# A gated delta rule layer with a mixture of experts on one core: how the first pairs of each inverse are selected, how its first two levels get their transposed halves, and a new order of work on all engines

## The reference

```
mixed = silu(causal_conv(x @ w_qkv, conv_w))         # 4 taps; q, k: 16 heads of 128; v: 32 heads of 128
z = x @ w_z;  beta = sigmoid(x @ w_b);  g = -exp(A_log) * softplus(x @ w_a + dt_bias)
q, k = l2norm(q) * 128**-0.5, l2norm(k)              # each key head serves two value heads
for t in range(512):                                 # per sequence and value head, state 128 x 128
    state = state * exp(g[t])
    delta = (v[t] - k[t] @ state) * beta[t]
    state = state + outer(k[t], delta)
    o[t] = q[t] @ state
o = rmsnorm(o * silu(z)) * gamma
x = layernorm(x + o @ w_out)
```

## Time and profile before

| what | value |
|---|---|
| median of three runs | 2604.27 us |
| the profiled execution | 2603.33 us |
| its span, first to last instruction | 2601.6 us |
| around the span | 1.7 us |
| mean granted clock of TensorE | 0.967 of full speed |
| busy: PE, DVE, POOL, ACT | 91%, 76%, 54%, 52% |

### The profile page before, as it was taken

How to read it: one execution, slowest core, us unless ns; L and a number is a source line. 1 busy time by engine, 2 the same in 40 slices (tenths; PEclk the granted TensorE clock), 3 DMA queues, 4 the chain that set the end, 5 groups by cost and what they waited for, 6 DMA issues and landing times.

```text
span 2601.6 us, 54037 instructions
## 1 busy us (share of the span) xinstructions
PE 2379.1 (91%) x20078; PEld 1827.1 (70%) x20078; DVE 1987.8 (76%) x3452; ACT 1359.8 (52%) x4123; POOL 1417.4 (54%) x1198
## 2 busy tenths in 40 slices
PE   5899999999999999999999999999999999997998
PEld 3677777777777777777777777777777777775665
DVE  4778778777887777877778777887778877784665
ACT  3555565555555555555555555555555555553110
POOL 3465655656555665556655566555666556662000
PEclk9899999999999999999999999999999999998999
DMA  3011010101010100101010101101010110001000
GB/s 125 34 42 34 33 42 34 42 34 47 28 50 25 50 34 26 50 29 46 34 42 34 46 29 35 41 34 50 26 50 26 50 34 26 34 2 71 25 9 17
DMA packets 32100, 98.47 MB, mean 38 GB/s; under 512 B 4320, under 2 KB 9824, under 8 KB 31584
## 3 DMA queue, kind: packets, MB, share of 16 engines
q1 hardware_dynamic: 31840, 95.02, 10.6%
HBM read 92.39 MB, written 2.62 MB: 37 GB/s over the span
## 4 chain that ended last, share of the span: by engine, by line
PE 70%; POOL 16%; DVE 8%; issue 4%; ACT 0%; POOLq 0%; DMA 0%; DVEq 0%; SPq 0%; ACTq 0%
PE bank L870 18%; POOL XT L810 11%; PE bank L894 11%; PE bank L992 4%; PE bank L924 4%; PE bank L965 4%; PE bank L914 4%; PE bank L991 4%; PE bank L482 4%; DVE X L1152 3%; PE bank L953 3%; POOL mhiT L796 3%; PE bank L975 2%; PE bank L930 2%; PE bank L878 2%
## 5 line engine op out<-in xcount | busy, mean ns | idle before, releaser
L1125 DVE SCALAR_TENSOR_TENSOR conv<-bank,cw_all,conv 128x511 f32<-128x511 f32 (+2 forms) x768 | 571.4, 744 | 19.6 <-ACT conv L1030 6.0
L870 PE MATMUL bank<-xT,w_kh 128*128 128x512 f32 x1024 | 537.7, 618 | 2.7 <-ACT kraw L1058 1.8
L1075 ACT ACTIVATE X<-bank 128x512 f16<-128x512 f32 x384 | 228.9, 596 | 449.2 <-PE bank L924 435.8
L1161 DVE TENSOR_TENSOR N<-bank,lev 128x512 f16<-128x512 f32 x384 | 264.8, 690 | 107.3 <-PE bank L914 97.6
L914 PEld LDWEIGHTS bank<-X,mhiT 128*128 128x128 f16 x3072 | 132.3, 98 | 262.8 <-DVE X L1152 179.6
L750 POOL TENSOR_SCALAR ss<-ssum 128x4 f32<-128x4 f32 x64 | 14.6, 228 | 544.2 <-ACT sqj L1052 544.2
L894 PE MATMUL bank<-w_kh,xT 128*128 128x256 f32 x1024 | 310.0, 442 | 0.0
L914 PE MATMUL bank<-X,mhiT 128*128 128x64 f16 x3072 | 154.3, 194 | 165.6 <-DVE X L1152 164.2
L810 POOL TENSOR_SCALAR_AFFINE_SELECT XT<-mhiT 128x1024 f16<-128x1024 f16 x64 | 287.2, 4487 | 4.4
L1007 PE MATMUL bank<-wo,ogT 128*128 128x256 f32 x1024 | 246.8, 384 | 0.0
L1152 DVE STREAM_TRANSPOSE X<-XT 128x1024 f16<-128x1024 f16 x64 | 79.7, 1245 | 208.4 <-POOL XT L815 208.4
(11 more groups left out here) (160 smaller groups left out, 5859.7 us busy)
## 6 DMA issues: line engine op xcount, KB each, us to landing
egb<-rows SPq DMA_DIRECT2D x64, 512.0 KB, 3.6
ecb<-rows SPq DMA_DIRECT2D x64, 512.0 KB, 3.7
w_kh<-w_heads SPq DMA_DIRECT2D x16, 768.0 KB, 4.8
wo_raw<-w_out SPq DMA_DIRECT2D x16, 256.0 KB, 5.1
xT<-x_cols SPq DMA_DIRECT2D x4, 512.0 KB, 5.9
qT<-x_rows SPq DMA_DIRECT2D x4, 512.0 KB, 3.6
xT<-gate_up SPq DMA_DIRECT2D x1, 2048.0 KB, 7.5
out<-og SPq DMA_DIRECT2D x4, 512.0 KB, 3.0
```

The source lines that it names most:

```text
L870: mm = pe.matmul(PB[j % 2][:, :], w[:, k, g * P:(g + 1) * P], xT[:, k, b * SEQ:(b + 1) * SEQ], start=(k == 0), stop=(k == KT - 1))
L1075: act.activation(blocks(X[:, :, :], i, 0), packed(IB[i % 2], i), ACT.Copy).then_inc(s_x, 1)
L1125: dve.scalar_tensor_tensor(conv[:, g, m:], PB[j % 2][:, 0:SEQ - m], cw_all[:, head, g * TAPS + 3 - m:g * TAPS + 4 - m], conv[:, g, m:], op ...
L1161: dve.tensor_tensor(blocks(N[:, i], i, 0), packed(IB[1 - i % 2], i), blocks(lev[:, 1 + i:2 + i, :], i, 0).broadcast_to(shape), ALU.mult).t ...
```

## The change

1. `pairs`: the first select wrote all columns of XT with a pattern of three dimensions whose innermost had two elements, and the second then put ones into the odd columns, after a wait on the first. Now two selects of 512 elements in each partition write the even and the odd columns from the matching columns of `mhiT`, with the comparison `is_ge` and fill 0. Neither reads what the other writes, and the semaphore between them is gone. `x0` waits for both. What stands in XT is the same as before.
2. `TURNED` goes from 2 to 0: at levels 0 and 1 the transposed half comes from `growt` on PE and ACT, and DVE's two transposes `turned` are gone.
3. `ORDER` is new on all four engines. PE's round now begins with `write` of chunk 0 and `products` 1. `products` 0 of body k + 2 is the last item of the round before, and `solve` 0 stands ahead of it. `m`, `mhi`, `pairs`, `x0` and `join` 0 have moved from the end of the round to its beginning (ahead 1 in place of 2), and `solve`, `read` and `write` of chunk 1 from the end of the round before to this one. The three gate items of a body but the first stand between `products` and `join` 0.

```diff
--- before.py
+++ after.py
@@ -24,40 +24,41 @@
 NX = NE + 1
 NQ = 4
 Q_BETA, Q_EG, Q_KEYS, Q_EEND = range(NQ)
-TURNED = 2
+TURNED = 0
 COLS_OF = (1, 0, 2, 3)
 
 ORDER = {
     "tensor": [
-        ("read", 2, 0), ("growx", 0, 1), ("gate", 1, 1), ("gate", 2, 1), ("join", 1, 1), ("gate", 3, 1),
-        ("growx", 1, 1), ("proj", 0, 2), ("proj", 1, 2), ("join", 2, 1), ("solve", 2, 0), ("proj", 2, 2),
-        ("growx", 2, 1), ("growt", 2, 1), ("proj", 3, 2), ("join", 3, 1), ("write", 2, 0), ("out", 0, 0),
-        ("growx", 3, 1), ("ktp", 0, 2), ("read", 3, 0), ("growt", 3, 1), ("join", 4, 1), ("out", 1, 0),
-        ("growx", 4, 1), ("solve", 3, 0), ("growt", 4, 1), ("out", 2, 0), ("join", 5, 1), ("out", 3, 0),
-        ("growx", 5, 1), ("growt", 5, 1), ("proj", 4, 2), ("newton", 0, 1), ("ktp", 1, 2), ("proj", 5, 2),
-        ("newton", 1, 1), ("finish", 0, 1), ("proj", 6, 2), ("finish", 1, 1), ("proj", 7, 2), ("solve", 0, 1),
-        ("products", 0, 2), ("write", 0, 1), ("products", 1, 2), ("turn", 0, 0), ("read", 1, 1), ("turn", 1, 0),
-        ("project", 0, 0), ("project", 1, 0), ("solve", 1, 1), ("project", 2, 0), ("project", 3, 0), ("vtp", 0, 2),
-        ("write", 1, 1), ("vtp", 1, 2), ("join", 0, 2), ("gate", 0, 2),
+        ("write", 0, 0), ("products", 1, 1), ("gate", 1, 1), ("read", 1, 0), ("gate", 2, 1), ("gate", 3, 1),
+        ("proj", 0, 2), ("solve", 1, 0), ("join", 0, 1), ("proj", 1, 2), ("write", 1, 0), ("growx", 0, 1),
+        ("growt", 0, 1), ("proj", 2, 2), ("read", 2, 0), ("proj", 3, 2), ("solve", 2, 0), ("join", 1, 1),
+        ("out", 0, 0), ("write", 2, 0), ("growx", 1, 1), ("growt", 1, 1), ("ktp", 0, 2), ("read", 3, 0),
+        ("join", 2, 1), ("out", 1, 0), ("solve", 3, 0), ("growx", 2, 1), ("out", 2, 0), ("out", 3, 0),
+        ("growt", 2, 1), ("join", 3, 1), ("proj", 4, 2), ("ktp", 1, 2), ("proj", 5, 2), ("growx", 3, 1),
+        ("growt", 3, 1), ("proj", 6, 2), ("join", 4, 1), ("proj", 7, 2), ("turn", 0, 0), ("growx", 4, 1),
+        ("growt", 4, 1), ("turn", 1, 0), ("project", 0, 0), ("join", 5, 1), ("project", 1, 0), ("growx", 5, 1),
+        ("growt", 5, 1), ("project", 2, 0), ("vtp", 0, 2), ("newton", 0, 1), ("newton", 1, 1), ("project", 3, 0),
+        ("finish", 0, 1), ("finish", 1, 1), ("vtp", 1, 2), ("gate", 0, 2), ("solve", 0, 1), ("products", 0, 2),
     ],
     "scalar": [
-        ("u", 1, 0), ("silu", 2, 1), ("silu", 3, 1), ("vals", 0, 1), ("vals", 1, 1), ("growx", 0, 1), ("zs", 0, 1),
-        ("growx", 1, 1), ("zs", 1, 1), ("tap", 0, 2), ("u", 2, 0), ("growx", 2, 1), ("growt", 2, 1), ("silu", 0, 2),
-        ("tap", 1, 2), ("growx", 3, 1), ("squares", 0, 2), ("growt", 3, 1), ("kraw", 0, 2), ("u", 3, 0),
-        ("growx", 4, 1), ("growt", 4, 1), ("power", 0, 0), ("growx", 5, 1), ("silu", 1, 2), ("growt", 5, 1),
-        ("squares", 1, 2), ("tap", 2, 2), ("power", 1, 0), ("u", 0, 1), ("tap", 3, 2), ("turn", 0, 0), ("turn", 1, 0),
+        ("growt", 4, 0), ("silu", 3, 1), ("growx", 5, 0), ("growt", 5, 0), ("vals", 0, 1), ("u", 0, 0),
+        ("vals", 1, 1), ("zs", 0, 1), ("zs", 1, 1), ("u", 1, 0), ("tap", 0, 2), ("growt", 0, 1), ("growx", 0, 1),
+        ("u", 2, 0), ("silu", 0, 2), ("tap", 1, 2), ("growx", 1, 1), ("growt", 1, 1), ("kraw", 0, 2),
+        ("squares", 0, 2), ("u", 3, 0), ("growx", 2, 1), ("power", 0, 0), ("silu", 1, 2), ("growt", 2, 1),
+        ("power", 1, 0), ("squares", 1, 2), ("tap", 2, 2), ("growx", 3, 1), ("growt", 3, 1), ("tap", 3, 2),
+        ("turn", 0, 0), ("growx", 4, 1), ("turn", 1, 0), ("silu", 2, 2),
     ],
     "vector": [
-        ("join", 2, 1), ("conv", 0, 2), ("conv", 1, 2), ("conv", 2, 2), ("join", 3, 1), ("s", 2, 0), ("conv", 3, 2),
-        ("join", 4, 1), ("rhs", 3, 0), ("og", 0, 0), ("conv", 4, 2), ("conv", 5, 2), ("join", 5, 1), ("scan", 0, 2),
-        ("scan", 1, 2), ("res", 0, 1), ("og", 1, 0), ("res", 1, 1), ("tt", 0, 1), ("tt", 1, 1), ("conv", 6, 2),
-        ("conv", 7, 2), ("conv", 8, 2), ("s", 0, 1), ("conv", 9, 2), ("m", 0, 2), ("m", 1, 2), ("rhs", 1, 1),
-        ("conv", 10, 2), ("conv", 11, 2), ("p", 0, 2), ("p", 1, 2), ("x0", 0, 2), ("acc", 0, 0), ("s", 1, 1),
-        ("join", 0, 2), ("rhs", 2, 1), ("turned", 0, 2), ("join", 1, 2), ("acc", 1, 0), ("turned", 1, 2),
+        ("m", 0, 1), ("m", 1, 1), ("s", 0, 0), ("p", 0, 1), ("p", 1, 1), ("rhs", 1, 0), ("x0", 0, 1), ("join", 0, 1),
+        ("s", 1, 0), ("conv", 0, 2), ("conv", 1, 2), ("rhs", 2, 0), ("conv", 2, 2), ("join", 1, 1), ("s", 2, 0),
+        ("conv", 3, 2), ("rhs", 3, 0), ("join", 2, 1), ("og", 0, 0), ("conv", 4, 2), ("conv", 5, 2), ("og", 1, 0),
+        ("join", 3, 1), ("conv", 6, 2), ("conv", 7, 2), ("join", 4, 1), ("conv", 8, 2), ("conv", 9, 2),
+        ("conv", 10, 2), ("join", 5, 1), ("conv", 11, 2), ("acc", 0, 0), ("scan", 0, 2), ("res", 0, 1), ("res", 1, 1),
+        ("tt", 0, 1), ("tt", 1, 1), ("scan", 1, 2), ("acc", 1, 0),
     ],
     "pool": [
-        ("eq", 0, 1), ("mlo", 0, 1), ("qe", 0, 1), ("keys", 0, 1), ("kn", 0, 2), ("diag", 0, 2), ("pow", 0, 0),
-        ("ogs", 0, 0), ("ogs", 1, 0), ("mhi", 0, 2), ("mhi", 1, 2), ("pairs", 0, 2),
+        ("mhi", 0, 1), ("mhi", 1, 1), ("pairs", 0, 1), ("qe", 0, 1), ("eq", 0, 1), ("mlo", 0, 1), ("keys", 0, 1),
+        ("kn", 0, 2), ("pow", 0, 0), ("ogs", 0, 0), ("ogs", 1, 0), ("diag", 0, 2),
     ],
 }
 
@@ -190,7 +191,6 @@
         s_mhi = sem("s_mhi")
         s_mdif = sem("s_mdif")
         s_mlo = sem("s_mlo")
-        s_near = sem("s_near")
         s_pair = sem("s_pair")
         s_x0 = sem("s_x0")
         s_np = sem("s_np")
@@ -807,13 +807,11 @@
                     pool.wait_ge(s_mhi, 2 * n + 2)
                     if n > 0:
                         pool.wait_ge(s_new, 2 * n)
-                    pool.affine_select(out=XT[:, :, :].rearrange("p x (b j) -> p x b j", j=2),
-                                       in_=mhiT[:, :, :].rearrange("p x (b j) -> p x b j", j=2), compare_op=ALU.is_equal, fill=0.0,
-                                       base=0, pattern=[[0, CELLS], [-2, P // 2], [0, 2]], channel_multiplier=1).then_inc(s_near, 1)
-                    odd = XT[:, :, :].rearrange("p x (b j) -> p x b j", j=2)[:, :, :, 1]
-                    pool.wait_ge(s_near, n + 1)
-                    pool.affine_select(out=odd, in_=odd, compare_op=ALU.not_equal, fill=1.0,
-                                       base=-1, pattern=[[0, CELLS], [-2, P // 2]], channel_multiplier=1).then_inc(s_pair, 1)
+                    for j in range(2):
+                        pool.affine_select(out=XT[:, :, :].rearrange("p x (b j) -> p x b j", j=2)[:, :, :, j],
+                                           in_=mhiT[:, :, :].rearrange("p x (b j) -> p x b j", j=2)[:, :, :, j],
+                                           compare_op=ALU.is_ge, fill=0.0, base=0, pattern=[[0, CELLS], [-2, P // 2]],
+                                           channel_multiplier=1).then_inc(s_pair, 1)
                 elif name == "pow":
                     if n == BODIES - 1:
                         for k in (1, 5):
@@ -1146,7 +1144,7 @@
                                       bank4(I1)[:, 2 * i:2 * i + 2].unsqueeze(2).broadcast_to([P, 2, VH, P]),
                                       half(decb, i).rearrange("p (c v) t -> p c v t", v=VH), ALU.mult).then_inc(s_p, 1)
                 elif name == "x0":
-                    dve.wait_ge(s_pair, n + 1)
+                    dve.wait_ge(s_pair, 2 * n + 2)
                     if n > 0:
                         dve.wait_ge(s_resp, 2 * n)
                     dve.transpose(flat(X), flat(XT)).then_inc(s_x0, 1)
```

## The result

The changed kernel takes 2402.23 us, the median of four runs (2401.18 to 2402.98), beside 2604.19 us for the kernel before on the same chip. The ratio is 0.9224 with a 95% interval of 0.9208 to 0.924. I had forecast 2440 us and a range of 2405 to 2525. The sign and the mechanism came out; the gain is 38 us larger than forecast and lies 3 us beyond the edge of the range.

The account below looks back on a forecast made before the run. PE bounds the kernel, with a 2.44 us stall and 1.08 us of clock loss in a 36.11 us round. A round of 33.5 us saves 63 x (36.11 - 33.5) = 164 us: 2440 us, range 2405 to 2525.

Parts of the forecast that it names:

- What bounds the kernel: PE sets the round of 36.11 us; 2.44 us of stall before the first `join` and 1.08 us of clock can be had.
- The selects: In `pairs` on POOL, each new select takes 0.755 us, in place of a wide one of 4487 ns and its follower.
- the open half of the bound: Upper bound of 2.24 us for a new select, half of line 810, should the comparison have made the wide one slow.
- The path to `join` 0: `m` to `x0` takes 5.0 to 5.1 us against 6.1 of PE work; about 1.0 us of slack, stall gone.
- The rival of slow selects: If `is_ge` costs as line 810, a select takes 2.24 us: 2633 us, slower from about 2.0 us a select; 8%.
- `growt` on PE: `growt` 0 and 1 add 0.23 us each to PE, 0.46 us a round.
- The clock: In the loop it stays at 1.00 once the stall is gone, worth the whole 1.08 us a round.
- The round, 33.5 us: One round of the loop: PE's own 33.1 us plus 0.4 us of waits, in place of 36.11.
- PE's own work, 32.6 us: PE's work in an undisturbed old round, 35.03 - 2.44, taken as confirmed by the busy time of 32.60.
- The 0.4 us of waits: Late items in the new round, such as `join` 4, `project` 0, `newton` and `solve` 0, together 0.4 us.
- The walk: Pass through all four engines' new lists for one round, each item timed after what it waits for; few found late.
- New waits: Rival: the new lists hide waits the forecast missed, one or two us more a round, 2503 or 2566 us; 17%.

Follow-up runs that it names:

- closer items: Kernel before with narrow selects in the old order, plus `newton` 0 and 1, `finish` 0 and 1, `growx` 4 and `growt` 4 adjacent on PE: 2411.85 us.

## Why the prediction came out as it did

**What bounds the kernel.** Right. The stall of 2.44 us before the first `join` and the clock's 1.08 us were all that could be had, and both came. The run with the selects alone shows the first and the two with repeated selects the second.

**The selects.** Right: 766 ns for 755. The comparison, the open half of the bound, has no effect.

**The path to `join` 0.** Right in kind, with 0.6 us of slack for 1.0. The DVE and POOL part was 0.1 us shorter than summed. PE's part was 5.7 us and not 6.1, because I had priced the items by the earlier trace rows, where the gate item stands behind an f16 `join` (0.94) and the `solve` is part 0 (0.60). In the new order the gates stand behind f32 items, and `solve` 1 takes 0.44: the line at 1210.17 has its successor 0.86 us later. The rival of slow selects had its turning point from that slack, so the point is nearer than I put it: 0.4 us less slack is 0.2 us for each select.

**`growt` on PE.** 0.46 us forecast, 0.48 measured.

**The clock.** Right: 1.00 in the loop. The two of three rounds with a fall that the prediction reckons from means are 36 of 63 when counted.

**The round, 33.5 us: this is the term that was mis-sized.** It is 32.86, and 63 x 0.64 = 40 us are the 38 that were missing, with the edges' 3 on the other side. Its two parts were both too large, the base by 0.2 us and the waits by almost all of their 0.4; 0.04 is rounding (32.6 + 0.46 + 0.4 is 33.46).

- *PE's own work, 32.6 us, was 0.2 too large.* I had subtracted the 2.44 us that the profile lists as idle. But that idle time starts only when the last matmul has drained. The item before the stall is this one, of the kernel before:

```profile
1253.22 0.60 PE L886 MATMUL bank<-tri_sb,vT 128*128 128x128 f32 x4
```

  Its successor would have started 0.44 us later, at 1253.66, and it started at 1256.27. The gap is 2.61 us, the work 35.03 - 2.61 = 32.42, and the run with the selects alone has a round of 32.41. The busy time of 32.60 that I took for a confirmation has the same drain in it, so it was no second source.
- *The 0.4 us of waits were added to a figure that held such waits already.* The walk found the right places: in the trace after, `proj` 6 and `join` 4 together start 0.34 us late (1228.57 to 1229.01 to 1230.08, where 0.23 and 0.94 are the steps without a wait). The old order has its own, of 0.1 us here and there, and these were part of "PE's own work". Only the difference of the two should have been added.
- *The new order has two passages from f16 to f32 matmuls fewer,* 14 for 16. Averaged over the undisturbed rounds of both orders, the gates, `solve` and `write` of a round, of which six parts now stand behind f32 items, are 0.48 us cheaper from start to start; `project` and `turn`, of which four now stand behind f16 ones, are 0.32 dearer, some waiting of their own included. That the passage is the reason is read from these steps and not shown by an experiment.

That new waits and saved passages nearly cancel is measured. The first rounds of a run, with a late first `x0` or a low clock, blur the mean over all 63, so here are the last 61 rounds of the changed kernel and of the old order with both other parts:

```profile
126.79:2134.01 2007.22, 2004.79 (x19400) 1609.81 (x19399) 1620.32 (x2746) 1267.99 (x3965) 1096.30 (x1114) 1.00 0.12 40
126.02:2129.91 2003.89, 2003.89 (x19400) 1599.88 (x19399) 1605.94 (x2747) 1312.76 (x3967) 1096.30 (x1114) 1.00 0.12 40
```

That is 32.91 us a round in the new order and 32.85 in the old one; the 32.86 and 32.89 of the table are these with the first rounds mixed in. So in place of 0.4 us the new order by itself adds 0.05. Its time is 7 us above the old order's, 2402.23 to 2395.44 from two sets of runs. The two profiled executions differ by 4.6 us, of which 3.3 are these rounds, 0.8 the rounds ahead of them and 0.5 what follows the last `x0`. The first `x0` is 6.1 us later in it (63.8 to 57.7), because `products` 0 stands behind `vtp` and `gate` 0 in the first round too, and `vtp` has to wait for `vT` there. I had put that delay at 3 us. By the third `x0` all but 0.8 us of the delay is made up.

**The rivals.** New waits did not outweigh; they appear at once when an order is disturbed, in the runs with the transposes in the new order and with closer items. The Trainium skill calls DVE's transpose the fastest for 32 x 32 blocks within a bank (VectorE: DVE Perf Modes, "Rules for kernel authors"). Which way is better for the kernel depends here on the order. In the old one DVE's transposes are the better choice, by 28 us, not because they are faster (1.24 us for 0.23 on PE and 0.49 on ACT) but because they leave PE alone, which is the bound. In the new one, at the places tried, they cost 98 us more. I had put the 0.46 us a round of `growt` into the sum and hadn't drawn the conclusion: the second and third part of the change take 34 us back, and the first alone is the best version.

**The range.** The forecast's own low end was a round of 32.9 us, and the range began at 2405 us. It left out what the prediction calls a walk that was too careful, and that is what came: the base could be high and was.

## What to carry to other kernels

When a wait is to vanish, measure the work that remains from start to start, and not by subtracting the idle time that a profile lists; and add to it only the difference between the new order's small waits and those the old one already had. When several edits come together, price each with the others left out: here one slow access pattern on a side engine was worth 236 us, and the two edits around it took 34 back. And look at rounds one by one before comparing means: a mean over all of them mixes the first rounds, and rounds at a lower clock, into a difference of hundredths. Work moved from an engine with room to the one that has become the bound costs its full time, even where it makes the path shorter.

## What the runs showed of the hardware

- A select on POOL over a pattern of three dimensions, the innermost two elements long, takes 4.48 us for 1024 f16 elements of each partition; two selects over every second element take 0.77 us each. With the other comparison they take 4.48 and 0.76 us. Which property of the wide pattern costs the time isn't separated.
- The clock of TensorE stayed at 2.4 GHz in all 63 rounds of 34 us with an idle time of 0.81 us before one `join` in each. With 2.32 us it fell to 1.2 GHz for a time in 46 of 63 rounds, with 2.44 us in the kernel before in 36, in the old order with `growt`, at the same total wait, in 52, and with 3.23 us in all 63. A round with one fall takes 1.6 us longer (36.63 for 35.03, 37.01 for 35.44, 37.09 for 35.52).
- An f32 item on PE that follows f16 matmuls takes 0.08 us longer to its successor than behind f32 ones (0.94 for 0.86, 0.52 for 0.44, 0.30 for 0.22); the transposes by matmul `ktp` 1 and `vtp` don't. This is read from timelines; no run isolates it.
